# A mixture of experts inside an attention stage: its tokens are scattered into blocks up front, or gathered and stored block by block through a table

## What is computed

```
def _moe(x, Wg, W1, b1, W2, b2):
    xf = x.reshape(S * B, D)                  # 2048 tokens of 128
    idx = jnp.argmax(xf @ Wg.T, axis=-1)      # one of 8 experts
    out = jnp.zeros_like(xf)
    for e in range(E):
        m = (idx == e)[:, None].astype(xf.dtype)
        h = jax.nn.relu(xf @ W1[e] + b1[e])   # 512 hidden
        out = out + m * (h @ W2[e] + b2[e])
    return out.reshape(S, B, D)
y = _layer_norm(x + _mha(x, Wqkv, bqkv, Wo, bo), g1, be1)
z = _layer_norm(y + _moe(y, Wg, W1, b1, W2, b2), g2, be2)
```

## Time and profile before

| | us |
|---|---|
| median of three runs | 1323.59 |
| lowest, highest | 1323.31, 1324.79 |
| span of the profiled execution | 1331.0 |

### The profile page before, as it was taken

One profiled execution on the slowest core, in us unless ns is written; L12 is line 12 of the kernel. 1 busy time (PEld: TensorE's weight loads), 2 busy tenths in 40 slices (PEclk: granted clock), 3 DMA queues, 4 the chain that ended last, 5 costly groups with the idle time before them and its releaser, 6 DMA issues. The chain is left out here.

```text
span 1331.0 us, 21677 instructions
## 1 busy us (share of the span) xinstructions
PE 1161.9 (87%) x6667; PEld 613.7 (46%) x6667; DVE 1103.2 (83%) x1535; ACT 1051.4 (79%) x1868; POOL 914.3 (69%) x749
## 2 busy tenths in 40 slices
PE   6566799999818999987999999999999999999885
PEld 4461144444414565663444444444444444444442
DVE  7966698999785323338999999999999999999997
ACT  4347799999743224359899999999999999999992
POOL 6734212111284442347999999999999999999995
PEclk9776799999966999998999999999999999999998
DMA  2122223433107305523345234423441444144420
GB/s 70 33 86 96 74 86 104 123 111 114 34 22 253 130 17 130 150 68 103 76 104 124 66 68 108 105 77 77 104 109 55 93 106 109 49 88 103 105 65 16
DMA packets 89061, 120.20 MB, mean 90 GB/s; under 512 B 17869, under 2 KB 49464, under 8 KB 88576
## 3 DMA queue, kind: packets, MB, share of 16 engines
q1 hardware_dynamic: 82688, 101.59, 30.0%
q0 software_dynamic: 6272, 17.38, 4.5%
HBM read 92.28 MB, written 27.45 MB: 90 GB/s over the span
## 5 line engine op out<-in xcount | busy, mean ns | idle before, releaser
L2094 POOL TENSOR_TENSOR hcm<-hs,Cc 128x1024 f32<-128x1024 f32 x255 | 600.8, 2379 | 27.5 <-DVE hs L2477 23.1
L2477 DVE TENSOR_TENSOR_SCAN hs<-decay,dbx 128x512 f32<-128x512 f32 x512 | 586.8, 1200 | 25.5 <-ACT decay L2370 9.5
L2211 PEld LDWEIGHTS dbx<-ident_sb,scaled 128*128 128x128 f32 x2048 | 227.7, 142 | 288.4 <-DVE hs L2477 164.4
L2211 PE MATMUL dbx<-ident_sb,scaled 128*128 128x128 f32 x2048 | 312.3, 283 | 41.4 <-DVE hs L2477 38.1
L2352 ACT ACTIVATE scaled<-duT,BT 128x256 f32<-128x256 f32 x579 | 266.9, 506 | 0.2 <-PE dbx L2211 0.2
L2370 ACT ACTIVATE decay<-dtr_even,a_all 128x512 f32<-128x512 f32 x256 | 178.6, 721 | 3.0 <-DVE hs L2477 1.7
L2370 ACT ACTIVATE decay<-dtr_odd,a_all 128x512 f32<-128x512 f32 x256 | 177.9, 721 | 2.3 <-DMA dtr_odd<-dt_turn 1.5
L929 ACT ACTIVATE ex<-tt 128x1024 f32<-128x1024 f32 x128 | 138.4, 1081 | 5.5 <-DVE tt L979 5.1
L2229 PE MATMUL y_bank<-hcm,fold_sb 128*32 128x512 f32 x1024 | 139.5, 617 | 2.1 <-POOL hcm L2094 2.1
L2142 PE MATMUL slots<-XT,w_tap 128*128 128x512 f32 (+1 forms) x224 | 115.4, 597 | 3.1 <-DVE scaled L2468 2.7
L978 DVE TENSOR_TENSOR tt<-bank_l,gt 128x512 f32<-128x512 f32 x128 | 87.4, 683 | 27.9 <-PE bank_l L823 19.2
(11 more groups left out here) (379 smaller groups left out, 1938.0 us busy)
## 6 DMA issues: line engine op xcount, KB each, us to landing
Cc<-bc_turn SPq DMA_DIRECT2D x256, 64.0 KB
dtr_even<-dt_turn SPq DMA_DIRECT2D x32, 512.0 KB, 8.6
dtr_odd<-dt_turn SPq DMA_DIRECT2D x32, 512.0 KB, 8.4
dt_turn<-dt SPq DMA_DIRECT2D x16, 512.0 KB, 2.8
hid<-in_conv_row SPq DMA_DIRECT2D x4, 512.0 KB, 5.9
shares_of_tokens<-zeros SPq DMA_DIRECT2D x2, 1024.0 KB, 8.1
w_rg<-in_w_rg SPq DMA_DIRECT2D x8, 256.0 KB
w_ru<-in_w_ru SPq DMA_DIRECT2D x8, 256.0 KB
```

The lines of the kernel that those rows point to most:

```text
L2094: nc.gpsimd.tensor_tensor(hcm[:, r - 1:r + 1, :], hs[:, p % HR - 1:p % HR + 1, :], Cc[:, k:k + 1, :].broadcast_to([P, 2, 512]), ALU.mult). ...
L2211: last = nc.tensor.transpose(dbx[bank_of[p]][:, P * kk:P * kk + P], scaled[buffer_of(l, b, k)][:, kk, g, :, :].rearrange("p j c -> p (j c) ...
L2477: nc.vector.tensor_tensor_scan(hs[:, p % HR, :], dec[:, p % DR, :], dbx[bank_of[p]][:, :], 0.0, ALU.mult, ALU.add).then_inc(s_sc, 1)
```

## The change

Rows are no longer scattered ahead and gathered at the end. `Y1` is stored plainly to `token_rows` in DRAM at the start of stage two. A table `rows_of` says for each lane of each block three numbers: the weight row, the row to read (token 0 where the lane is unfilled) and the row to write (past the end where unfilled, and then dropped). To make it, VectorE splits each token's place into block and lane (steps 4, 10, 11 and 12), POOL makes 0-and-1 patterns of them (`in_block` times the token's number plus one, `on_lane`), TensorE multiplies these at step 17 (`find_tokens`, 16 products), and VectorE copies the table from its bank at step 19. In the loops POOL then gathers a block's rows by the table, gathers its weights, and stores each result by the table to `token_outs` at the tokens' own rows. SP keeps the loads of operands and passes on that a store has landed (`s_free`). Stage three loads `token_outs` plainly, in four loads on SP.

The diff, with declarations and unchanged lines cut:

```diff
@@ -88,13 +88,12 @@
...
     wo_att = sb(keep0, "wo_att_sb", [P, D])
-    row_u = sb(keep0, "row_u", [P, NT], u32)
...
     AHEAD = 2
-    yx_dram = nc.dram_tensor("block_rows", [(BLOCKS + AHEAD) * P, D], fp32).ap()
-    yo_dram = nc.dram_tensor("block_outs", [BLOCKS * P, D], fp32).ap()
+    tok_dram = nc.dram_tensor("token_rows", [T, D], fp32).ap()
+    acc_dram = nc.dram_tensor("token_outs", [T, D], fp32).ap()
     qk_dram = nc.dram_tensor("qk_parts", [2, 3, P, T], bf16).ap()
@@ -642,8 +641,17 @@
...
         eo = [sb(st2, f"block_out{i}", [P, D]) for i in range(2)]
-        at_w = [sb(st2, f"weight_rows{i}", [P, 1], u32) for i in range(2)]
-        zeros = sb(st2, "zeros2", [P, (BLOCKS + AHEAD) // 2, D])
+        at = [sb(st2, f"weight_and_token_rows{i}", [P, 1, 3], u32) for i in range(4)]
+        rows_of = sb(st2, "rows_of_blocks", [P, BLOCKS + AHEAD, 3])
+        unfilled = sb(st2, "unfilled", [P, BLOCKS])
+        lane_row = sb(st2, "lane_row", [P, P])
+        lane_of = sb(st2, "lane_of", [P, NT])
+        token_no = sb(st2, "token_no", [P, NT])
+        lane16 = sb(st2, "lane16", [P, 1])
+        firsts = sb(st2, "first_rows", [P, BLOCKS + AHEAD])
+        from_on = sb(st2, "from_on", [P, NT, BLOCKS + AHEAD])
+        in_block = sb(st2, "in_block", [P, NT, BLOCKS])
+        on_lane = sb(st2, "on_lane", [P, NT, P])
         below = sb(st2, "below2", [P, P])
...
@@ -692,53 +700,39 @@
...
                     sp.dma_start(dst, src).then_inc(s_cst, 16)
-                sp.wait_ge(s_zz, 1)
-                half = P * (BLOCKS + AHEAD) // 2
-                for i in range(2):
-                    sp.dma_start(yx_dram[half * i:half * i + half, :].rearrange("(p k) d -> p k d", p=P), zeros[:, :, :]).then_inc(s_zf, 16)
-
-                def load_block(j, i):
-                    sp.dma_start(xb[i][:, :], yx_dram[bass.ds(j * P, P), :]).then_inc(s_xl[i], 16)
+                sp.dma_start(tok_dram.rearrange("(p t) d -> p t d", t=NT), Y1[:, :, :]).then_inc(s_tok, 16)
+                sp.sem_inc(s_free, LEAD)
...
                         sp.wait_ge(s_L, step(q, 0))
-                        sp.wait_ge(s_zz, 1)
+                        sp.wait_ge(s_ones, 1)
                     load_part(sp, q * 2 + 3, 1, part, s_ld[1])
...
                         sp.wait_ge(s_L, step(q, 16))
-                        sp.wait_ge(s_zz, 1)
+                        sp.wait_ge(s_ones, 1)
                     load_part(sp, q * 2 + 4, 0, part, s_ld[0])
...
                     load_part(sp, 1, 1, part, s_ld[1])
-                sp.wait_ge(s_scat, 16 * NT)
-                for i in range(AHEAD):
-                    load_block(i, i)
                 for part in range(2):
...
                     for k in range(PER):
-                        if more or k + AHEAD < PER:
-                            sp.wait_ge(s_xt, blk(q, k + 1))
-                            sp.wait_ge(s_zz, 1)
-                            load_block(q * PER + (k + AHEAD), k % 2)
                         if k < 2:
...
                             first_head_of_next(q, k - 4)
-                        sp.wait_ge(s_ek, blk(q, k + 1))
-                        sp.wait_ge(s_zz, 1)
-                        sp.dma_start(yo_dram[bass.ds((q * PER + k) * P, P), :], eo[k % 2][:, :]).then_inc(s_es[k % 2], 16)
+                        sp.wait_ge(s_es[k % 2], loaded(q, k))
+                        sp.sem_inc(s_free, 1)
...
                 turn(2, False)
-                for i in range(2):
-                    sp.wait_ge(s_es[i], 16 + loaded(2, PER - 2))
@@ -748,12 +742,21 @@
...
-                def gather_weights(q, j, i, n):
-                    nc.gpsimd.tensor_copy(at_w[i][:, :], w_row[:, bass.ds(j, 1)]).then_inc(s_cur, 1)
+                def gather_block(q, j, i, n):
+                    r = at[n % 4]
+                    nc.gpsimd.tensor_copy(r[:, :, :], rows_of[:, bass.ds(j, 1), :]).then_inc(s_cur, 1)
                     pool.wait_ge(s_cur, blk(q, n + 1))
                     pool.sem_inc(s_asked, 1)
-                    nc.gpsimd.indirect_dma_start(weights[i][:, :], None, A["w_expert"], bass.IndirectOffsetOnAxis(ap=at_w[i][:, 0:1], axis=0),
+                    nc.gpsimd.indirect_dma_start(xb[i][:, :], None, tok_dram[:, :], bass.IndirectOffsetOnAxis(ap=r[:, 0, 1:2], axis=0),
+                                                 bounds_check=T - 1, oob_is_err=False).then_inc(s_xl[i], 16)
+                    nc.gpsimd.indirect_dma_start(weights[i][:, :], None, A["w_expert"], bass.IndirectOffsetOnAxis(ap=r[:, 0, 0:1], axis=0),
                                                  bounds_check=NE * P - 1, oob_is_err=False).then_inc(s_wl[i], 16)
+                def store_block(q, k):
+                    pool.wait_ge(s_ek, blk(q, k + 1))
+                    pool.sem_inc(s_asked, 1)
+                    nc.gpsimd.indirect_dma_start(acc_dram[:, :], bass.IndirectOffsetOnAxis(ap=at[k % 4][:, 0, 2:3], axis=0), eo[k % 2][:, :], None,
+                                                 bounds_check=T - 1, oob_is_err=False).then_inc(s_es[k % 2], 16)
@@ -770,17 +773,26 @@
...
                     values_of(i, i)
-                nc.gpsimd.memset(zeros[:, :, :], 0.0).then_inc(s_zz, 1)
                 pool.sem_inc(s_cur, LEAD)
-                pool.wait_ge(s_rows, 1)
-                pool.wait_ge(s_zf, 32)
+                link = Chain(pool, s_pch)
+                PT = nc.gpsimd.tensor_tensor
+                pool.wait_ge(s_cst, 16 * 4)
+                link(nc.gpsimd.tensor_scalar(lane16[:, :], lane[:, :], float(NT), 1.0, ALU.mult, ALU.add))
+                link(nc.gpsimd.tensor_scalar(token_no[:, :], starts[:, :], 1.0 / P, None, ALU.mult))
+                link(nc.gpsimd.tensor_scalar(token_no[:, :], token_no[:, :], lane16[:, 0:1], None, ALU.add))
+                link(nc.gpsimd.tensor_scalar(firsts[:, :], blocks[:, :], float(P), None, ALU.mult), s_hot)
+                pool.wait_ge(s_lanes, 1)
+                link(PT(in_block[:, :, :], from_on[:, :, 0:BLOCKS], from_on[:, :, 1:BLOCKS + 1], ALU.subtract))
+                link(PT(in_block[:, :, :], in_block[:, :, :], token_no[:, :].unsqueeze(2).broadcast_to([P, NT, BLOCKS]), ALU.mult))
+                pool.wait_ge(s_lanes, 2)
                 for t in range(NT):
-                    nc.gpsimd.indirect_dma_start(yx_dram[:, :], bass.IndirectOffsetOnAxis(ap=row_u[:, t:t + 1], axis=0), Y1[:, t, :], None,
-                                                 bounds_check=(BLOCKS + AHEAD) * P - 1, oob_is_err=False).then_inc(s_scat, 16)
+                    last = nc.gpsimd.tensor_scalar(on_lane[:, t, :], lane_row[:, :], lane_of[:, t:t + 1], None, ALU.is_equal)
+                link(last, s_hot)
                 pool.wait_ge(s_rows, 2)
+                pool.wait_ge(s_tok, 16)
                 for i in range(AHEAD):
-                    gather_weights(0, i, i, i)
+                    gather_block(0, i, i, i)
                 next_head(-1, 0)
@@ -790,7 +802,9 @@
...
                             pool.wait_ge(s_dn, blk(q, k + 1))
-                            gather_weights(q, q * PER + (k + AHEAD), k % 2, k + AHEAD)
+                            pool.wait_ge(s_free, blk(q, k - 1))
+                            gather_block(q, q * PER + (k + AHEAD), k % 2, k + AHEAD)
+                        store_block(q, k)
                     if more:
@@ -829,12 +843,19 @@
...
                     nc.tensor.matmul(rank_bank[:, 0:P], ones[:, :], cum[0][:, 0:NT, :].rearrange("p t e -> p (t e)"), start=False, stop=True)
+                    nc.tensor.matmul(rank_bank[:, 2 * P:3 * P], ones[:, :], below[:, :], start=True, stop=True)
                     nc.tensor.matmul(rank_bank[:, P:P + NE], ones[:, :], cum[0][:, NT, :], start=True, stop=True).then_inc(s_rk, 1)
+                def find_tokens():
+                    pe.wait_ge(s_hot, 2)
+                    for t in range(NT):
+                        last = nc.tensor.matmul(bank_e[:, 0, 0:BLOCKS], on_lane[:, t, :], in_block[:, t, :], start=(t == 0), stop=(t == NT - 1))
+                    last.then_inc(s_tk, 1)
...
                     pe.wait_ge(s_ek, blk(q, k))
-                    pe.wait_ge(s_rows, 1)
+                    pe.wait_ge(s_rows, 2)
                     nc.tensor.transpose(bank_e[:, 0, :], xb[k % 2][:, :], ident[:, :]).then_inc(s_xt, 1)
@@ -881,6 +902,8 @@
...
                             rank_tokens()
+                        if first and st == 17:
+                            find_tokens()
                         if mb == 0 and not (first and u < 2):
@@ -939,7 +960,7 @@
...
                     act.wait_ge(s_dn, blk(q, k + 1))
-                    act.wait_ge(s_es[k % 2], loaded(q, k))
+                    act.wait_ge(s_free, blk(q, k - 1))
                     nc.scalar.activation(eo[k % 2][:, :], bank_e[:, 0, :], ACT.Copy).then_inc(s_ek, 1)
@@ -1021,19 +1042,31 @@
...
                         link(TT(tiles[:, 2, :], tiles[:, 1, :], tiles[:, 0, :], ALU.subtract))
```

(28 more changed lines are left out.)

8 lines of the change are left out of this document (3 added, 5 removed).

## The result

The changed kernel takes 1337.26 us (median, 1335.38 to 1339.59), the kernel before 1324.19 beside it: a ratio of 1.0095, 95% interval 1.008 to 1.011. The forecast was 1314.5, in a range of 1310 to 1327.

What follows compares the result with a forecast made beforehand. It took ScalarE's tanh and exponential to bound the attention loops, with a ScalarE gap in the first pair. For the median, -4.3 + 1.0 + 2.3 - 8.1 = -9.1 gave 1314.5 us, range 1310 to 1327.

Steps and rivals of the forecast that it cites:

- Stage three, -4.3: Stage three: four plain loads on SP replace 16 gathers by POOL, ending VectorE's waits for gathers; gain 4.3 us.
- the three waits: Stage three: VectorE's sums waited for gathers 1.12, 1.99 and 1.22 us, 4.33 us in all.
- VectorE's added steps, +1.0: First pair of heads: VectorE's new steps come to 1.8 us, partly covered by ScalarE's work; cost 1.0 us (0.5 to 1.8).
- The table, +2.3 with no wait for POOL: First pair: TensorE's 32 passes cost 2.3 us beyond cover at the high clock level, POOL's comparisons being done in time.
- The rival with that wait: First pair: TensorE reaches the table before POOL's comparisons end, then works at the low clock; +7.6 us, 1331.2; chance 0.14.
- The loops, nothing: Loops over heads: POOL's added load and store and SP's later operands cost nothing while the margins hold.
- the bound on POOL that I had as a rival: Loops: POOL's three issues per block exceed 7.45 us, deciding at 1.9 us each; about 1343 us; chance 0.06.
- The stage's end, nothing: End of stage two: one unit's weighing, turning and sum cover the last store's landing; no cost.
- The gap, -8.1: First pair, 127 to 145 us: ScalarE's 11.8 us gap goes with the scatters; gain 8.1 us in the median run.
- that rival: First pair: the gap stays or is not in the runs; 1322.6 us, or 1326.3 at the low clock; chance 0.35.

Runs made afterwards that it cites:

- the table in one piece: The changed kernel with TensorE's table at step 22 in place of 17 and its reading by VectorE at step 24 in place of 19: ratio 1.0061.
- the second profile of before: The kernel before profiled once more with no edit: span 1320.4 us.

## Why the prediction was wrong, point by point

- **Stage three, -4.3: right in the sum, partly by luck.** The plain loads are worth 5.7 us where they are the only edit, more than the three waits that I added up; in the changed kernel the products for the biases, 2.1 us slower, bring that back to -4.0.
- **VectorE's added steps, +1.0: too much.** With the table in parts the first pair is 0.6 us shorter than before; ScalarE's work covers them there.
- **The table, +2.3 with no wait for POOL: the step that failed most.** The rival with that wait had a chance of 0.14, was to decide from 0.38 us per comparison, and was priced at 7.6 us in all. The comparisons took 0.58 us, within my bounds of 0.3 to 0.64; they began at 129.50 (I had 131.0) and ended at 138.82, while TensorE asked at 135.2 (I had 137.1). The nearest row, 0.47 us for a step over 256 elements, already lay above 0.38, and I still took no wait; a comparison over 128 took longer than that step over 256. The first pair is 9.1 us longer than in the kernel before. Without a wait the table in one piece cost 5.3, between my 2.3 at the high level and 6.0 at the low, and the clock fell there too: that TensorE keeps the high level once the gap is gone was not right either.
- **The loops, nothing: failed, +6.0 in this trace (+1.9 at the least in others),** not by the bound on POOL that I had as a rival (issues stayed at 1.0 to 1.4 us), but by two margins. For operands I had the second half leave some 4 us later; it left 7.6 us later (219.94 for 212.37), and both kinds were late, the next pair's at 230.5 and a second head's at 322.7. I let a store land 2.3 us behind its issue by a row without other traffic; the median is 3.9, the longest 7.2. The Trainium skill (DMA: Bandwidth & Descriptors, Anatomy of one DMA — SWDGE (gpsimd) path) gives a transfer issued by GpSimd 2.0 us and its bytes over 436 GB/s, an estimate of 2.15 us for 64 KB; that agrees with the shortest landing, 2.1, alone. For weights I took the margin from a block without POOL's copies for the next head, 8.5 us from asking to use; blocks 6 and 14 had 6.9, and there the weights, asked for among SP's operand loads, took 7.4 and 7.8 us to land. The cost of that meeting of two queues had no term.
- **The stage's end, nothing: failed, +2.9.** I covered the store's landing; what counts is POOL's 6.20 us behind its last indirect transfer, which moving SP's wait does not touch and moving the store does. The prediction had no term for it.
- **The gap, -8.1: failed.** The runs of the kernel before hold little or none of it: 70 of them beside the experiments took 1321.41 to 1330.70 us, less than that execution's 1332.9, and the one traced has no gap. I had most of the number for it: the profiled span's excess over the median was 7.4 us, 9.3 with the 1.9 that a time has over its span, of the 11.8. The excess spoke for the low end, and I took the middle. The Trainium skill's rule beside that rival (Runtime: NRT & Kernel Launch, Instruction fetch mechanics) by which the gap would stay is not borne out: the gap did not come back, nor is its cause shown.
- The rule beside the rival on POOL (SBUF — State Buffer, SBUF: two separate sides, of the Trainium skill; 3.1 us for a transfer held up by VectorE) is not what these runs show: 72 issues in the changed kernel's first pair and loops took 0.98 to 1.38 us with VectorE busy 90% of the time. (The page has it for some VectorE operations only; whether these are among them is not shown.)

Summed by the stages of the trace: -0.8 + 9.1 + 6.0 + 2.9 - 4.0 + 2.5 = +15.7 against the second profile of before. That run took 1322.18 us, 2.0 below the median beside which the change was timed, and the profile after lies 0.7 above its own; so the runs show +13.1. Of the 2.5 us in the rest, which the change does not touch, 1.4 lie in TensorE's last products: 4.0 us of wait for them in the changed kernel, 2.6 before, at granted clocks of 0.50 and 0.92 in the last 8 us. Other changed kernels have a rest of 925.5 to 927.3, kernels before 923.7 to 925.3; why was not settled.

## What to carry to other kernels

A helper engine's work that must be done before TensorE's next instruction in order is a wait on everything behind it; give it slack, or cut TensorE's share into parts that each step covers. When stores move to another queue, follow every semaphore that waits for a landing, for each load behind it, with the landing as measured among the new traffic. And if one profiled execution is longer than the timed runs, look first for the stretch that it alone has, before counting on getting it back.

## What the runs showed that I had not expected

- POOL's first instruction of the next stage comes 6.20 to 6.21 us behind an indirect transfer that ends its stage (seven kernels; 6.50 where rows are asked for at the turn), whoever waits for the landing. Where the trace has that transfer's landing, it is 2.1 us behind its issue, long before.
- A wait of TensorE can cost more than itself, where the granted clock falls behind it. In the loops waits for a DMA of 1.97, 2.26 and 2.54 us made a block 3.6 to 3.8 us longer, each with a granted clock of 0.50 behind it; of eleven waits of 1.05 to 1.58 us, ten cost about themselves at an unchanged 1.00, and one of 1.52 made a block 3.0 longer. After 3.69 us the table's passes took 7.02 us, against four parts of 1.07.
- Weights asked for by POOL among SP's operand loads came later (6.1 to 7.8 us, not 4.1 to 5.9, in the changed kernel's loops; 9.3 with twelve loads in one block). With the loads in two blocks and the rows asked for at the turn, TensorE had no wait for weights (three traces).
